# Cross-attention on one core: two weighings behind each other in one row of products, their outputs made together, and 24 more identity transposes in the prologue

## The reference

```python
x = x + _L0_xattn_ref(_layernorm(x), ctx_1024, Wq, Wk, Wv, Wp, bp)
# in it:  q = split(x @ Wq); k = split(y @ Wk); v = split(y @ Wv)
#         attn = softmax(q k^T * HEAD_DIM ** -0.5);  out = (attn @ v) @ Wp + bp
x = x + _L0_attn_ref(_layernorm(x), ...)     # self-attention over 64 tokens, with a bias
x = x + _L0_ffn_ref(_layernorm(x), ...)      # squared ReLU, spike count
```

## Time and profile before

| | |
|---|---|
| median of 3 runs | 1816.08 us |
| profiled execution | 1815.34 us, span of its instructions 1813.5 us |
| mean granted TensorE clock | 0.998 of full speed |
| PE busy | 1795.0 us (99% of the span) |
| DVE, ACT, POOL busy | 1304.9, 827.1, 898.7 us |
| PE idle before its instructions, longest | 2.3 us (once), 1.5 us (once), 1.4 us (once) |

### The profile page before, as it was taken

The page is one execution under the profiler, slowest core; times in us unless marked ns, Lnnn a source line. Parts: engine busy times, 40 slices in busy tenths (PEclk is TensorE's granted clock), DMA queues, the critical chain, the costliest instruction groups (busy, mean ns, idle before and its releaser), DMA issues. The chain is left out here.

```text
span 1813.5 us, 65800 instructions
## 1 busy us (share of the span) xinstructions
PE 1795.0 (99%) x28780; PEld 1561.4 (86%) x28780; DVE 1304.9 (72%) x1942; ACT 827.1 (46%) x982; POOL 898.7 (50%) x824
## 2 busy tenths in 40 slices
PE   9999999999999999999999999999999999999998
PEld 8979898989898989898988888888888877778887
DVE  6865959596968687777868696969696957574265
ACT  4643545454545444444545454535354523344232
POOL 0443737373737373746464655556464744344111
PEclk9999999999999999999999999999999999999999
DMA  6210202020202020202011110202020232123110
GB/s 259 112 49 3 84 4 83 3 84 3 83 3 84 3 84 3 84 3 83 12 75 34 53 57 30 80 7 84 3 84 2 75 107 76 25 87 108 40 59 24
DMA packets 43360, 101.20 MB, mean 56 GB/s; under 512 B 19121, under 2 KB 20657, under 8 KB 42961
## 3 DMA queue, kind: packets, MB, share of 16 engines
q1 hardware_dynamic: 43088, 96.88, 15.3%
HBM read 86.48 MB, written 8.29 MB: 52 GB/s over the span
## 5 line engine op out<-in xcount | busy, mean ns | idle before, releaser
L556 POOL TENSOR_TENSOR fold<-fold,prob 128x256 f32<-128x256 f32 x698 | 705.8, 1011 | 55.2
L114 PE MATMUL ring<-y_parts,w_keep 128*128 128x402 f32 (+1 forms) x3072 | 607.5, 351 | 1.4 <-PEq L192 1.4
L114 PEld LDWEIGHTS ring<-y_parts,w_keep 128*128 128x128 f32 x3072 | 551.6, 188 | 15.6 <-issue 2.3
L114 PE MATMUL ring<-wv_s,y_parts 128*128 128x512 f32 x2304 | 545.1, 395 | 0.0
L114 PEld LDWEIGHTS ring<-wv_s,y_parts 128*128 128x128 f32 x2304 | 430.7, 188 | 98.7
L550 POOL TENSOR_TENSOR fold<-prob 128x256 f32<-128x256 f32 x64 | 80.7, 1261 | 622.1 <-ACT prob L610 621.9
L579 ACT ACTIVATE k_sb<-ring 128x402 f32<-128x402 f32 (+1 forms) x256 | 129.4, 506 | 361.9 <-PE ring L114 361.9
L770 DVE TENSOR_TENSOR prob<-prob,peak_rows 128x1024 f32<-128x1024 f32 (+1 forms) x192 | 261.6, 1415 | 1.6
L604 ACT ACTIVATE prob<-s_ps 128x1536 f32<-128x1536 f32 (+1 forms) x128 | 200.0, 1562 | 127.9 <-PE s_ps L919 127.9
L735 DVE TENSOR_TENSOR fold<-fold,prob 128x512 f32<-128x512 f32 x192 | 172.9, 901 | 79.7 <-ACT prob L604 73.9
L610 ACT ACTIVATE prob<-prob 128x1024 f32<-128x1024 f32 (+1 forms) x192 | 210.8, 1125 | 7.4 <-DVE prob L770 5.1
(11 more groups left out here) (214 smaller groups left out, 1629.6 us busy)
## 6 DMA issues: line engine op xcount, KB each, us to landing
y_raw<-yT SPq DMA_DIRECT2D x48, 804.0 KB, 7.2
y_raw<-yT SPq DMA_DIRECT2D x16, 792.0 KB, 9.9
f_raw<-w_ffn SPq DMA_DIRECT2D x22, 512.0 KB, 3.6
v_sb<-y_left SPq DMA_DIRECT2D x1, 2304.0 KB, 11.3
v_sb<-v_left SPq DMA_DIRECT2D x16, 130.0 KB
p_x<-x SPq DMA_DIRECT2D x4, 512.0 KB, 6.3
q_scratch<-p_x SPq DMA_DIRECT2D x8, 256.0 KB, 2.1
q_sb<-q_scratch SPq DMA_DIRECT2D x16, 128.0 KB, 9.2
```

Source lines behind the costliest of these rows:

```text
L114: mm = pe.matmul(out, left(a, c), right(b, c), start=(c == 0 and n == 0), stop=(c == DC - 1 and n == 2))
L556: pool.tensor_tensor(acc[0:m], acc[0:m], prob[0:m, i, t, :], ALU.add).then_inc(sum_step, 1)
```

## The change

In `batch`, the weighings of blocks 0 and 1 of the batch before now stand behind each other, and so do those of blocks 2 and 3, in two neighbouring parts of `small_ps`. Their outputs are made in one RECIPROCAL and one multiplication for both. Keys, scores, copies, exponentials and DVE's work are reordered around them. In the last batch only blocks 0 and 1 stand together. The prologue has 56 identity transposes at its head, 8 after `turn(0)` and 8 at its end.

```diff
-        WARM = 48
+        WARM, BETWEEN = 56, 8
...
+            def warm(bank, times):
+
+                for n in range(times):
+                    pe.transpose(bank[:, n % DC * P:(n % DC + 1) * P], ident[:], ident[:])
+
+            warm(t_ps[3], WARM)
             turn(0)
+            warm(q_bank[NBLK - 1], BETWEEN)
             first_queries(range(NBLK - 1))
             turn(1)
             queries(range(NBLK - 1, NQ))
+            warm(t_ps[3], BETWEEN)
...
+        def weighed(i):
+            return small_ps[:, (i % 2) * 2 * N:(i % 2 + 1) * 2 * N]
...
+                key(b, 2, 0)
+                exponential(b, 0, 0)
+                key(b, 2, 1)
+                score(b, 1, 0)
+                exponential(b, 0, 1)
+                key(b, 2, 2)
+                score(b, 1, 1)
+                exponential(b, 0, 2)
+                key(b, 2, 3)
+                key(b, 3, 0)
+                score(b, 2, 0)
...
+            def outputs(b, i):
+                blocks = NBLK * b + i + 2
+                both = small_ps[:, 0:4 * N].rearrange("p (k z n) -> p k z n", k=2, z=2)
+                dve.wait_ge(pv_ok, blocks)
+                dve.reciprocal(rec[:], both[:, :, 1, :]).then_inc(rec_ok, 2)
+                dve.wait_ge(rec_ok, blocks)
...
+                dve.tensor_tensor(o_sb[:, i:i + 2, :], both[:, :, 0, :], rec[:], ALU.mult).then_inc(o_out, 2)
...
                 if past:
-                    output(b - 1, 0)
+                    outputs(b - 1, 0)
...
                 for i in (1, 2):
-                    if past:
-                        output(b - 1, i)
                     row_of_peaks(b, i - 1)
                     subtract(b, i - 1)
+                    if past and i == 1:
+                        outputs(b - 1, 2)
                     largest(b, i, 0)
...
-                if past:
-                    output(b - 1, 3)
...
+            def two_weighings(b, i):
+                small_read(b, i - 1)
+                weigh(b, i, weighed(i))
+                weigh(b, i + 1, weighed(i + 1))
+
+            def batch(b, past, last=False):
+                keys(b, 0, 0)
+                keys(b, 0, 1)
+                if past and not last:
+                    two_weighings(b - 1, 0)
+                keys(b, 0, 2)
+                keys(b, 0, 3)
...
+                keys(b, 1, 0)
+                scores(b, 0, 0)
+                keys(b, 1, 1)
+                scores(b, 0, 1)
+                keys(b, 1, 2)
+                keys(b, 1, 3)
...
+                elif past:
+                    two_weighings(b - 1, 2)
+                keys(b, 2, 0)
...
+                keys(b, 2, 1)
+                scores(b, 1, 0)
+                keys(b, 2, 2)
+                scores(b, 1, 1)
+                keys(b, 2, 3)
+                keys(b, 3, 0)
+                scores(b, 2, 0)
+                keys(b, 3, 1)
+                scores(b, 2, 1)
+                keys(b, 3, 2)
+                keys(b, 3, 3)
```

More of the change, by code:

```diff
@@ L386, in _ @@
             pe.wait_ge(ident_ok, 2)
-            for n in range(WARM):
-                pe.transpose(t_ps[3][:, n % DC * P:(n % DC + 1) * P], ident[:], ident[:])
+            def warm(bank, times):
+                for n in range(times):
+                    pe.transpose(bank[:, n % DC * P:(n % DC + 1) * P], ident[:], ident[:])
+            warm(t_ps[3], WARM)
             turn(0)
+            warm(q_bank[NBLK - 1], BETWEEN)
             first_queries(range(NBLK - 1))
@@ L420, in cross_attention @@
         peak = sb("peak", [P, HQ // SQ])
-        rec = sb("rec", [P, N])
+        rec = sb("rec", [P, 2, N])
         o_sb = sb("o_sb", [P, NBLK, N])
@@ L630, in keys_phase @@
                     value_weights()
[L631 to L645, removed]
+                key(b, 1, 0)
+                score(b, 0, 0)
+                key(b, 1, 1)
+                score(b, 0, 1)
+                key(b, 1, 2)
+                key(b, 1, 3)
+                if not past:
+                    for j in range(LEFT_SLOTS):
+                        left_high(j)
+                key(b, 2, 0)
[9 more added lines that the diff above has]
+                score(b, 2, 0)
+                key(b, 3, 1)
+                score(b, 2, 1)
+                key(b, 3, 2)
+                exponential(b, 1, 0)
+                exponential(b, 1, 1)
+                key(b, 3, 3)
+                exponential(b, 1, 2)
                 if not past:
@@ L770, in subtract, with output @@
                     dve.tensor_tensor(piece(i, n), piece(i, n), row(n), ALU.subtract).then_inc(sub_ok, 1)
-            def output(b, i, at=small_ps, share=rec[:]):
+            def outputs(b, i):
[4 more added lines that the diff above has]
+                dve.wait_ge(rec_ok, blocks)
+                if i == 0:
+                    reached(dve, o_stored, 16 * b)
+                dve.tensor_tensor(o_sb[:, i:i + 2, :], both[:, :, 0, :], rec[:], ALU.mult).then_inc(o_out, 2)
+            def output(b, i, at, share):
                 block = NBLK * b + i
@@ L809, in keys_phase @@
                     largest(b, i, 1)
-                if past:
-                    output(b - 1, 3)
-                else:
+                if not past:
                     for j in range(LT):
@@ L925, in small_read, with weigh @@
                 reached(pe, o_out, NBLK * b + i + 1)
-            def weigh(b, i, at=small_ps, summed=JT):
+            def weigh(b, i, at, summed=JT):
                 block = NBLK * b + i
@@ L949, in weigh @@
                 mm.then_inc(pv_ok, 1)
[L951 to L965, removed]
+            def two_weighings(b, i):
[9 more added lines that the diff above has]
+                keys(b, 0, 3)
+                if last:
+                    two_weighings(b - 1, 0)
+                keys(b, 1, 0)
[4 more added lines that the diff above has]
+                keys(b, 1, 3)
+                if last:
+                    small_read(b - 1, 1)
+                    weigh(b - 1, 2, weighed(2))
+                elif past:
+                    two_weighings(b - 1, 2)
+                keys(b, 2, 0)
+                if last:
+                    weigh(b - 1, 3, weighed(3))
+                keys(b, 2, 1)
[9 more added lines that the diff above has]
+                keys(b, 3, 3)
                 if not past:
@@ L992, in _ @@
                 batch(b, True)
-            batch(B - 1, True)
+            batch(B - 1, True, True)
             out_ahead(0)
```

## The result

The changed kernel takes 1844.15 us (median of 6 runs, 1842.75 to 1845.89). The kernel before, on the same chip, took 1816.16 us (6 runs, 1812.78 to 1817.59). The ratio is 1.0159, 95% interval 1.0147 to 1.0171: slower by 28 us, far outside the predicted range of 1808.4 to 1829.4. The profiled execution has a span of 1843.1 us, 29.6 more than before.

A forecast was written before the change was run, and what follows sets the result against it. PE, busy 1795.0 of 1813.5 us, was taken to bound the kernel. Joined weighings -9.0, tile 7 wait +9.8, batch 0 +0.8 and prologue +0.5 gave +2.1 us on 1816.08: 1818.2 us, range 1808.4 to 1829.4.

The forecast's parts named there:

- The gain: PE's loop: each weighing directly behind another saves 0.31 us of boundaries, 29 times, -9.0 us in all.
- The wait at value tile 7: PE waits for DVE's copy of value tile 4, 0.65 us in each of batches 1 to 15, +9.8 us.
- DVE's chain: DVE from block 1's second scores to the end of value tile 4's copy: 35.1 us, bounds 34.2 and 37.1.
- Batch 0: Block 0's exponentials stand on ACT ahead of block 1's first score copy, so second scores start late: +0.8 us.
- The prologue: Ahead of the loop: 8 more transposes before `turn(0)` delay it, +0.5 us.
- rival (4): PE's gap in a weighing near the end may stay, go or double: up to 4 us either way, range only.
- the one that costs the last 8 transposes at nothing: End of prologue: the last 8 transposes lie where PE waits for other engines, costing nothing; without that cover 0.9 us.
- DVE's output pair: Stands before largest 1, where DVE waits for scores anyway: costs the chain nothing; about 1.4 us without that cover.
- No change: Own case, within 0.2%: a PE wait of 0.25 to 0.8 us a batch, net -4 to +4 us; chance 0.35.

The follow-up runs named there:

- repaired kernel: Changed kernel with old prologue, context loads held, batch 0 in its old order and value tile 4 copied inside largest 3: 1808.97 us, 0.9957 of the kernel before.
- the kernel with both undone: Changed kernel with the earlier prologue (48 transposes) and SyncE's context loads held until the first scores of block 3: 1817.53 us, 1.0013 of the kernel before.
- the two kernels with the old prologue: Changed kernel with the earlier 48-transpose prologue: 1826.28 us as is, 1817.53 us with context loads also held until the first scores of block 3.
- the last three kernels of the new order: The kernel with both undone, 1817.53 us; the repaired kernel, 1808.97; the latter with the late load of x's rows held until weighing (15,1) is done, 1804.87.
- early loads: Kernel before, with the context loads issued about 28 us into the batch instead of 57: 1837.69 us, ratio 1.0119.

## Why the prediction was wrong

**The gain was right in kind and size.** Forecast 0.31 us for each joined weighing, 0.62 a batch. The repaired kernel's undisturbed batch is 88.05 - 87.35 = 0.70 shorter, and a pair takes 3.27 us (forecast 3.3). 29 of them are the -9.0 forecast.

**The wait at value tile 7 was right in place, and priced too high.** In the kernel with both undone, tile 7 starts 0.50 us behind the matmul before it and not 0.23: a wait of 0.27, not 0.65, so +4 and not +9.8 over 15 batches. DVE's chain there, in the batch from 233.41:

```profile
272.53 2.77 DVE L759 TENSOR_TENSOR fold<-fold,prob 128x512 f32<-128x512 f32 x3 [2.68 <-ACT prob L616]
...
306.65 0.68 DVE L731 COPY v_sb<-ring 128x512 f32<-128x512 f32 x1
```

From 272.53 to 307.33 are 34.8 us (35.1 forecast; 35.5 in the batch shown of the changed kernel). PE, without a wait, would reach tile 7 37.9 us behind the start of block 1's second scores (37.8 forecast). Both terms were good to 0.3 us; but the wait is the small difference of two long stretches, and 0.3 is half of it. In the changed kernel gap B delays PE ahead of tile 7 and hides most of it.

**Batch 0.** Forecast +0.8 for late second scores. The new order costs 2.3 us there (107.4 and 107.5 in the two kernels with the old prologue), in another place: DVE's left halves come late (L733). The step that priced batch 0 looked only at ACT's copies. The changed kernel adds a packet gap of 1.82 us, and its clock falls behind each of the two gaps (below), which makes 7.5.

**The prologue.** Forecast +0.5, measured +1.07. Part of this is the execution and not the transposes: with them the loop starts at 39.02, 38.25 and 38.46 us in three traces; in the six with neither transposes nor waits added it starts between 37.95 and 38.36.

**The step that failed** is rival (4), the sentence "The instruction stream is laid out anew, so this 4 us may stay, go or double", and the one that costs the last 8 transposes at nothing. Both take the layout as a thing that happens once. In a loop of 14 rounds a packet end at the wrong place is paid for in nearly every one: the transposes cost the old order 19.4 us over batches 1 to 14 (1252.24, 1232.88 before). **The second fault** is an omission: the prediction lists what DVE's output pair does to DVE and PE, and never what stands behind the outputs in SyncE's queue. It should have followed the store, and the loads behind it, 22 us forward into narrow blocks. That is gap B, 10 us alone. No change, which had 0.35, is near the truth for the new order with its loads held (1.0013), partly by luck: batch 0 and small packet gaps made up for the wait that was priced too high. It is wrong for the kernel as changed.

The Trainium skill bears on both, page "Runtime: NRT & Kernel Launch", section "Instruction fetch mechanics". It says that instructions are refilled in blocks of 16 KiB, 256 instructions, over a DMA queue that the sequencer drives itself. The rows agree: 256 packets with 4.19 MB together, and gaps at one remainder by 256. It calls the cost of crossing a block "mostly hidden". Here that holds over wide products, and fails in narrow blocks with the DMA engines full (gaps of up to 2.7 us), behind the loop's head (up to 1.1), and in the joined weighings with the DMA engines nearly idle (up to 0.5). It also says that a taken branch to a page outside the window makes execution wait for a fetch. The trace agrees in part. Gap A is in 13 of 14 batches, and the one without it, batch 1, is the only one that is entered from straight code and not by the jump back. But PE does not wait at the jump: a packet moves some 3 us ahead of it, and PE stops 28 instructions further on, for the next one.

**Still open.** Beside a large load the packets start late and take no longer; what holds back their start, no run shows, nor what fills the 1.2 to 1.7 us between a packet's end and PE's going on. Gaps at 3288, in the joined weighings, remain in four or five batches of the last three kernels of the new order, with no large load under way. The two faults together cost 2 us more than singly, which is about what the medians of the kernel before differ from chip to chip (1814.59 to 1816.17).

## What to carry to other kernels

When a bracket says "issue", or names an engine that was not late, look for the packets of the instruction queue just ahead of the gap, and count PE's instructions: if the gaps stand multiples of 256 apart, the instruction stream is late. Here, moving a large load by a few us, or the loop by a few instructions, was worth more than the reordering at hand. Before moving a store or an output, follow the DMA queue behind it and ask what lies under the loads that come with it: here wide products bore them, and narrow blocks didn't. Adding or removing prologue instructions ahead of a loop is a change to the loop.

## What was not expected of the hardware

24 transposes ahead of a loop cost 19 us inside it; 48 instructions of waits alone cost it 17 (1249.70 us for batches 1 to 14), and 256 instructions cost the loop half a us. Waits that are satisfied are not free: 414 of them, 208 instructions, held PE for 19.8 us; in the trace one starts 106 ns behind the other.

No gap in the loop lowered the granted clock (1.8 us at most, with early loads). Longer ones did in some executions and not in others: in the changed kernel the clock fell behind the wait of 2.07 us in batch 0, and in the kernel with both undone it stayed full behind the same wait of 2.02 us and behind the gap of 2.3 us at 9944. Windows of the changed kernel: the first holds gap B, the second lies behind the gap of 1.82 us in batch 0, the third behind the wait of 2.07 us.

```profile
286.00:300.00 14.00, 13.42 (x259) 11.27 (x257) 13.46 (x22) 7.59 (x8) 6.92 (x8) 1.00 0.02 4
...
57.00:61.00 4.00, 4.00 (x19) 3.85 (x20) 1.69 (x3) 1.66 (x1) 0.00 (x0) 0.58 0.27 109
...
97.00:101.00 4.00, 3.80 (x10) 2.99 (x11) 2.48 (x4) 0.00 (x0) 3.65 (x4) 0.61 0.53 197
```

0.58 and 0.61 are stretches mostly at the lower of the two levels (1.2 GHz); 0.42 x 4 + 0.39 x 4 = 3.2 us are lost besides the 3.9 of the gaps themselves, near all of batch 0's +7.5.
